# Attention loop of a gated block: TensorE's side work split into halves over two steps, with a new step table

## The chip, the cores and the metric

The kernel runs on one core of a Trainium2 chip. The metric is the device time of one execution in microseconds (us). All times below are in us unless marked ns. The engines are TensorE (PE; its weight loads are PEld), VectorE (DVE), ScalarE (ACT), GpSimd (POOL) and SyncE (SP, which issues most of the DMAs).

## What is computed

```python
x = x + tanh(g_xattn) * attention(layernorm(x), ctx, ctx, Wq, Wk, Wv, Wo)   # 16 heads, 512 queries, 1601 keys
x = x + tanh(g_ffn) * moe(layernorm(x), router_w, w1, w2)                    # top 2 of 8 experts

# attention: the softmax runs over the queries (axis=2), then each row is divided by its sum over the keys
attn = einsum("bhnc,bhlc->bhnl", qh * scale, kh)
attn = softmax(attn, axis=2)
attn = attn / sum(attn, axis=-1, keepdims=True)
out = einsum("bhnl,bhlc->bhnc", attn, vh)
```

x is 8 x 512 x 256, ctx is 8 x 1601 x 256, everything in float32.

## The kernel before

It has two phases. The first, `attention_and_routing`, takes the 8 batches one after the other; the second, `experts`, runs 71 blocks of 128 routed rows through their expert. The change touches the first alone.

**Steps.** A batch has 52 steps (`STEPS` = 4 groups of 4 heads x 13 tiles of 128 keys). A step has two units, one for each pair of heads. For a unit TensorE computes two scores tiles of 128x512 (L549) into one of three slots of PSUM; VectorE takes their negated maximum over the queries (L810); ScalarE computes the two exponentials with their sums (L659). Once a step VectorE takes the reciprocals of the four sums (L796), GpSimd scales the values with them (L934), and TensorE adds the weighted values into `acc` (L562), two steps behind the scores. The scores of a unit wait for the exponentials of the unit three before it.

**Side work.** TensorE also has 31 "fills" per batch, each into the one PSUM bank `spare`, and each in the step that the table `FILL_AT` gives it, between the scores of the step's first and second unit. "next" fills prepare the following batch: `k` 0 to 7 and `q` 0 and 1 are projections of two fp32 matmuls (L493, L483), `v` 0 to 6 projections of four (L499; the last has two), `x_turn` are transposes of x (L478). "tail" fills finish the batch before: `o_turn` 3, `attn_turn` 1, `out_proj` 0 and 1 (eight PE instructions each at L512), `row_turn`, `logits`, `prefix`. "cur" fills belong to the batch itself. In the loop over batches the first has no tail and the last has no next; b is 0 to 7.

**Who empties the bank.** A fill waits until the fill before it has been taken (`fill_taken`). `k` and `q` are taken by ScalarE at the start of their step, before the step's first exponential (L606, high part as bf16), then by VectorE after the maximum of the step's second unit (L711, remainder), and by GpSimd (two more parts, the last one a step later). `v` and `x_turn` are taken by ScalarE at the start of the step (L615, L619). `o_turn`, `attn_turn`, `out_proj` (L726), `row_turn`, `logits` and `prefix` are taken by VectorE between the maxima of the step's first and second unit.

**Queues.** The parts of k and q go to DRAM through two buffers in turn: SyncE stores them (L359, L354), and ScalarE's high part of a chunk waits until the store of the chunk two before has landed. SyncE's queue is in order: at the start of a batch it issues 16 loads of the fourth group's operands (L366, L368), then the stores of k 0 to 3, the store of x2, the stores of k 4 to 7, loads of x, the store of q 0, the loads for group 1 of the next batch, the store of q 1, the loads for groups 2 and 3, and last the load of the context of the batch after the next (L379), which waits until `v` 6 has been taken. `k` 0 waits for that load. For the first batch the loads of groups 2, 3 and 4 stand together ahead of the store of its k 0.

Of the kernel before, what the change touches and what calls it, by code (L numbers as in the profile page):

```python
# [40 lines left out]
KC = D // P  # L41
NT = N // P
LT = (L + P - 1) // P
# [23 lines left out]


FILL_AT = {
    2: ("next", "k", 0), 3: ("tail", "o_turn", 3), 4: ("next", "k", 1), 5: ("tail", "attn_turn", 1),  # L70
    6: ("tail", "out_proj", 0), 7: ("next", "k", 2), 8: ("tail", "out_proj", 1), 9: ("next", "k", 3),
    11: ("next", "k", 4), 13: ("next", "k", 5), 15: ("next", "k", 6), 16: ("cur", "o_turn", 0),
    17: ("tail", "row_turn", 0), 18: ("tail", "row_turn", 1), 20: ("tail", "logits", 0), 21: ("next", "k", 7),
    22: ("next", "x_turn", 0), 23: ("next", "x_turn", 1), 24: ("next", "q", 0), 26: ("next", "q", 1),
    28: ("next", "v", 0), 29: ("next", "v", 1), 30: ("cur", "o_turn", 1), 31: ("next", "v", 2),
    33: ("next", "v", 3), 35: ("next", "v", 4), 36: ("tail", "prefix", 0), 37: ("next", "v", 5),
    39: ("next", "v", 6), 42: ("cur", "o_turn", 2), 43: ("cur", "attn_turn", 0),
}


FIRST_FILL_AT = {s + 21: ("next", name, i) for s, (name, i) in enumerate(
# [2 lines left out]
ORDER = [KC + i for i in range(KC * KCHUNK)] + list(range(KC))  # L84
FIRST_ORDER = [KC + i for i in range(KCHUNK)] + [0] + [KC + i for i in range(KCHUNK, 2 * KCHUNK)] + [1]
EARLY = KCHUNK + 1
LOGITS = 20
ROUTE = 23
PLACE = 37
OUT = 8  # L90
STATS_X = (7, 11, 12, 13)
CENTRE_X = 16


class Iteration:
# [22 lines left out]
    def fill(self, s):  # L118

        if s not in self.table:  # L120
            return None
        kind, name, i = self.table[s]
        return (name, i) if {"tail": self.tail, "cur": self.cur, "next": self.next}[kind] else None

    def two_banks(self, name, i):

# [61 lines left out]
def attention_and_routing(nc, keep, x, ctx_t, g_xattn, g_ffn, wq_t, wk_t, wv_t, wo_t, router_t,  # L188
# [7 lines left out]
    with ExitStack() as ctx:  # L196
# [265 lines left out]
        def _(pe):  # L462
            pe.wait_ge(constants, 1)

            def fill(it, name, i):
                b = it.b
                spare = bank(it, name, i)
                if it.two_banks(name, i):

                    wait(pe, fill_taken, it.made(name, i) - 2)  # L470
                elif name != "logits":

                    wait(pe, fill_taken, it.made(name, i) - 1)
                if name == "x_turn":

                    pe.wait_ge(xn_ready, 2 * (b + 2))
                    for t in range(NT):
                        mm = pe.transpose(spare[:, t * P:(t + 1) * P], x_in[:, t, i * P:(i + 1) * P], ident[:, :])  # L478
                elif name == "q":
                    if it.first and i == 0:  # L480
                        pe.wait_ge(weights_in, N_WEIGHTS * 16)
                    for k in range(KC):
                        mm = pe.matmul(spare[:, :], wq_sb[:, k, i * P:(i + 1) * P], x_t[:, k, :],  # L483
                                       start=(k == 0), stop=(k == KC - 1))
                elif name == "k":
                    m, c = i // KCHUNK, i % KCHUNK
                    if it.first and i == 0:

                        pe.wait_ge(wk_in, 16)
                    if i == 0:  # L490
                        pe.wait_ge(ctx_loaded, (b + 2) * 16)
                    for k in range(KC):
                        mm = pe.matmul(spare[:, 0:KCOLS[c + 1] - KCOLS[c]], wk_sb[:, k, m * P:(m + 1) * P],  # L493
                                       ctx_sb[:, k, KCOLS[c]:KCOLS[c + 1]], start=(k == 0), stop=(k == KC - 1))
                elif name == "v":
                    for lt in range(2 * i, min(2 * i + 2, LT)):
                        r = rows_of(lt)
                        for k in range(KC):
                            mm = pe.matmul(spare[0:r, (lt % 2) * D:(lt % 2 + 1) * D], ctx_sb[:, k, lt * P:lt * P + r],  # L499
                                           wv_sb[:, k, :], start=(k == 0), stop=(k == KC - 1))  # L500
                elif name == "o_turn":

                    pe.wait_ge(acc_taken, b * G + i + 1 if i < G - 1 else b * G)
                    for t in range(NT):
                        mm = pe.transpose(spare[:, t * P:(t + 1) * P], o_acc[:, t * P:(t + 1) * P], ident[:, :])
                elif name == "attn_turn":
                    for t in range(NT):
                        mm = pe.transpose(spare[:, t * P:(t + 1) * P], attn[:, t, i * P:(i + 1) * P], ident[:, :])
                elif name == "out_proj":
                    for t in (2 * i, 2 * i + 1):  # L510
                        for k in range(KC):
                            mm = pe.matmul(spare[:, (t % 2) * D:(t % 2 + 1) * D], attn_t[:, k, t * P:(t + 1) * P],  # L512
                                           wo_sb[:, k, :], start=(k == 0), stop=(k == KC - 1))
                elif name == "row_turn":

                    pe.wait_ge(rows_ready, 2 * b)
                    for t in range(NT):
                        mm = pe.transpose(spare[:, t * P:(t + 1) * P], routed_rows[:, 0, t, i * P:(i + 1) * P], ident[:, :])
                elif name == "logits":
                    for t in range(NT // 2, NT):  # L520
                        for k in range(KC):
                            mm = pe.matmul(spare[:, t * E:(t + 1) * E], row_t[:, k, t * P:(t + 1) * P],
                                           router_sb[:, k, :], start=(k == 0), stop=(k == KC - 1))
                else:

                    pe.wait_ge(route_step, b * ROUTE_STEPS)
                    pe.matmul(spare[:, 0:NT * E], tri[:, :], chosen[:, :, :], start=True, stop=False)
                    mm = pe.matmul(spare[:, 0:NT * E], ones[:, :], seen_at[:, :, :], start=False, stop=True)
                mm.then_inc(fill_ready, 1)

            def first_logits(it):

# [33 lines left out]
            def run(it):  # L566
                for s in range(STEPS):
                    if s == SLOTS // 2 and it.cur and isinstance(it.b, int) and it.b == 0:

                        pe.wait_ge(fill_taken, it.base)  # L570
                    if it.cur:
                        unit_scores(it.b, s, 0)
                    if it.fill(s):
                        fill(it, *it.fill(s))
                    if it.tail and s == LOGITS - 1:
                        first_logits(it)
                    if it.cur:
                        unit_scores(it.b, s, 1)
                    if s >= 2 and it.cur:
                        weigh(it.b, s - 2)  # L580
                    if s < 2 and it.tail:
                        weigh(it.b - 1, STEPS + s - 2)
# [678 lines left out]
```

## Time and profile before

| what | value |
|---|---|
| median of 3 runs | 1903.37 us (1903.24 to 1906.2) |
| profiled execution | 1903.8 us, its span 1902.0 us |
| PE busy | 1672.8 us, 88% of the span |
| DVE busy | 1407.2 us, 74% |
| ACT busy | 1289.1 us, 68% |
| POOL busy | 557.8 us, 29% |
| batch loop | from 56 us to 1311 us |
| expert phase | to the end of the span |

The shares are means over two phases with different limits: in the second half of the span PE alone is busy nearly all the time, in the batch loop three engines are. A stretch of the loop is read from a table of windows, which has the busy time of each engine in it.

### The profile page before, as it was taken

The numbers are of one execution on the slowest core, as the hardware profiler recorded it, in microseconds if no ns is written. First come the engines' busy times: TensorE is split into PE (matmuls) and PEld (weight loads), VectorE is DVE, ScalarE is ACT, GpSimd is POOL, SyncE is SP. The second block draws the span as 40 slices with busy tenths as digits, with TensorE's granted clock in tenths as the row PEclk, the third lists the DMA queues.
The fourth block names the chain that finished last, engine by engine and source line by source line (L and its number), as shares of the span: only waits on it lengthen the run. The fifth ranks groups of instructions, "written<-read, shape, count | busy, mean of one in ns | idle before, by whom it ended". The sixth has DMA issues, their size and how long they took to land. (4 is left out here: it accounts for less than half of the span.)

```text
span 1902.0 us, 31292 instructions
## 1 busy us (share of the span) xinstructions
PE 1672.8 (88%) x9774; PEld 889.5 (47%) x9888; DVE 1407.2 (74%) x2269; ACT 1289.1 (68%) x3634; POOL 557.8 (29%) x837
## 2 busy tenths in 40 slices
PE   5589899889988989989988898886299999999997
PEld 3223233233323323323322332212299999999997
DVE  1488999999989999899998999996344444444443
ACT  2499989989999998999999999995011111111111
POOL 5141152235135135223413512213212222222222
PEclk9799999999999999999999999998599999999999
DMA  5915414432522441532343152114512222222221
GB/s 152 228 35 142 120 56 117 119 89 85 155 80 71 136 130 51 133 121 77 97 143 80 56 150 73 45 67 157 198 31 36 36 36 36 38 34 38 36 36 28
DMA packets 124933, 168.64 MB, mean 89 GB/s; under 512 B 14320, under 2 KB 102256, under 8 KB 124816
## 3 DMA queue, kind: packets, MB, share of 16 engines
q1 hardware_dynamic: 102064, 136.77, 26.1%
q0 software_dynamic: 13344, 17.90, 5.5%
q10 hardware_dynamic: 9408, 12.58, 1.8%
q8 instruction: 53, 0.87, 0.2%
q14 instruction: 64, 0.52, 0.1%
HBM read 117.96 MB, written 49.24 MB: 88 GB/s over the span
## 5 line engine op out<-in xcount | busy, mean ns | idle before, releaser
L659 ACT ACTIVATE w_all<-scores,negmax 128x512 f32<-128x512 f32 (+1 forms) x1664 | 1120.3, 717 | 48.6 <-DVE negmax L810 42.4
L810 DVE TENSOR_REDUCE negmax<-scores 128x2 f32<-128x1024 f32 (+1 forms) x832 | 1000.6, 1215 | 105.0 <-PE scores L549 100.4
L549 PE MATMUL scores<-q_stack,w_all 128*128 128x512 bf16 (+1 forms) x1550 | 477.8, 385 | 131.6 <-ACT w_all L659 114.2
L562 PE MATMUL acc<-w_all,vz 128*32 128x512 f32 (+1 forms) x3328 | 445.0, 607 | 8.8 <-POOL vz L934 7.7
L549 PEld LDWEIGHTS scores<-q_stack,w_all 128*128 128x128 bf16 (+1 forms) x1664 | 112.8, 100 | 605.4 <-ACT w_all L659 460.1
L659 ACT ACTIVATION_READ_ACCUMULATOR w_all<-scores,negmax 128x1 f32 (+1 forms) x1664 | 393.0, 236 | 0.0
L1128 ACT ACTIVATE hidden<-ps_hidden 128x512 f32<-128x512 f32 x142 | 84.8, 597 | 430.0 <-PE ps_hidden L1091 430.0
L934 POOL TENSOR_TENSOR vz<-w_all,rz 128x68 f32<-128x68 f32 (+1 forms) x416 | 124.6, 299 | 835.3 <-DVE rz L796 816.6
L1091 PEld LDWEIGHTS ps_hidden<-rows_t,w_sb 128*128 128x128 f32 x2272 | 267.4, 194 | 5.7 <-DVE rows_t L1155 1.7
L1091 PE MATMUL ps_hidden<-rows_t,w_sb 128*128 128x128 f32 x2272 | 268.2, 277 | 1.1 <-DVE rows_t L1155 1.0
L1104 PE MATMUL ps_y<-w_sb,hidden 128*128 128x256 f32 x1136 | 256.8, 379 | 0.0
L1206 POOL DMA_INDIRECT out<-result,gate_token x71 | 119.5, 1683 | 415.5 <-DVE result L1168 406.2
L1104 PEld LDWEIGHTS ps_y<-w_sb,hidden 128*128 128x128 f32 x1136 | 210.4, 190 | 25.7
L562 PEld LDWEIGHTS acc<-w_all,vz 128*32 128x32 f32 (+1 forms) x3328 | 65.5, 108 | 188.2 <-issue 117.0
L1161 DVE COPY gate_token<-rows 128x2 f32<-128x2 f32 x71 | 12.0, 170 | 181.2 <-DMA out<-result,gate_token 181.2
L493 PE MATMUL spare<-w_all,wk_sb 128*128 128x400 f32 (+1 forms) x240 | 94.0, 515 | 16.7 <-DMA w_all<-in_ctx_t 15.2
L1168 DVE TENSOR_SCALAR result<-ps_y,gate_token 128x256 f32<-128x256 f32 x71 | 34.4, 484 | 96.3 <-PE ps_y L1104 96.3
L1145 DVE COPY w_sb<-w_all 128x2048 f32 x71 | 86.9, 1224 | 14.5 <-POOLq L1199 14.2
L499 PE MATMUL spare<-wv_sb,w_all 128*128 128x256 f32 (+1 forms) x392 | 93.5, 380 | 2.1 <-DVE resid L711 1.5
L1150 DVE COPY w_sb<-w_all 128x2048 f32 x71 | 86.5, 1218 | 0.0
L499 PEld LDWEIGHTS spare<-wv_sb,w_all 128*128 128x128 f32 (+1 forms) x392 | 72.6, 186 | 19.1 <-DVE resid L711 2.3
L992 POOL DMA_INDIRECT routed<-routed_rows,place x64 | 65.0, 1015 | 28.8 <-DVE token L789 15.3
(134 smaller groups left out, 1008.2 us busy)
## 6 DMA issues: line engine op xcount, KB each, us to landing
w_all<-k_parts SPq DMA_DIRECT2D x256, 200.1 KB, 3.5
q_stack<-q_parts SPq DMA_DIRECT2D x256, 64.0 KB, 3.3
w_all<-in_ctx_t SPq DMA_DIRECT2D x8, 1601.0 KB, 7.9
k_parts<-parts SPq DMA_DIRECT2D x42, 300.0 KB, 2.8
w_all<-in_w ACTq DMA_DIRECT2D x12, 1024.0 KB, 12.0
rows<-routed SPq DMA_DIRECT2D x71, 129.0 KB, 2.0
q_parts<-parts SPq DMA_DIRECT2D x14, 384.0 KB, 3.1
k_parts<-parts SPq DMA_DIRECT2D x14, 300.8 KB, 3.0
```

Of the source, the lines that this page charges most:

```text
L493: mm = pe.matmul(spare[:, 0:KCOLS[c + 1] - KCOLS[c]], wk_sb[:, k, m * P:(m + 1) * P], ctx_sb[:, k, KCOLS[c]:KCOLS[c + 1]], start=(k == 0), ...
L499: mm = pe.matmul(spare[0:r, (lt % 2) * D:(lt % 2 + 1) * D], ctx_sb[:, k, lt * P:lt * P + r], wv_sb[:, k, :], start=(k == 0), stop=(k == KC ...
L549: mm = pe.matmul(scores[0:r, 2 * (u % SLOTS) + j % 2, :], k_stack[:, g, j, lt * P:lt * P + r], q_stack[:, g, j, :], start=True, stop=True)
L562: mm = pe.matmul(acc[32 * j:32 * j + 32, :], vz[0:r, s % RING, j, :], probs[0:r, s % RING, j, :], start=(lt == 0), stop=(lt == LT - 1))
L659: e = act.activation(probs[0:r, s % RING, j, :], scores[0:r, 2 * (u % SLOTS) + j % 2, :], ACT.Exp, bias=negmax[0:r, u % 4, j % 2:j % 2 + 1 ...
L810: dve.tensor_reduce(negmax[0:r, u % 4, :], scores[0:r, 2 * (u % SLOTS):2 * (u % SLOTS) + 2, :], AX.X, ALU.max, negate=True).then_inc(negma ...
L934: pool.tensor_tensor(vz[0:r, s % RING, :, 0:DH + 1], v_ones[0:r, b % 2, lt, g * GH:(g + 1) * GH, :], rz[0:r, s % RING, :].unsqueeze(2).to_ ...
L1091: mm = pe.matmul(ps_hidden[:, slot * BANKS + h // HB, (h % HB) * BLK:(h % HB + 1) * BLK], w1_sb[:, slot, k * HID + h * P:k * HID + (h + 1) ...
L1104: mm = pe.matmul(ps_y[:, slot, 0:D], hidden[:, slot, h * BLK:(h + 1) * BLK], w2_sb[:, slot, h * D:(h + 1) * D], start=(h == 0), stop=(h == ...
L1145: dve.tensor_copy(w1_sb[:, slot, :], w1_all[:, bass.ds(e * (KC * HID), KC * HID)]).then_inc(w1_ready, 1)
L1150: dve.tensor_copy(w2_sb[:, slot, :], w2_all[:, bass.ds(e * (HC * D), HC * D)]).then_inc(w2_ready, 1)
L1206: pool.indirect_dma_start(out=out, out_offset=bass.IndirectOffsetOnAxis(gate_token[:, slot, 1:2].bitcast(U32), 0), in_=result[:, slot, :], ...
```

## The change

The fills `k`, `q`, `v` (all but the last) and `out_proj` are issued in two halves: the first in the step before the one of the table, the second in the step of the table, each between the two units' scores. The wait for the bank stands before the first half. The first pass (b = -1, which has no attention beside it) keeps whole fills. The table is new: `k` 0 and 1 move from steps 2 and 4 to 1 and 3, `out_proj` from 6 and 8 to 7 and 9, `k` 2 to 5 from 7, 9, 11 and 13 to 11, 13, 15 and 18, `k` 6 and 7 from 15 and 21 to 24 and 26, `q` from 24 and 26 to 31 and 33, `v` 0 to 6 from 28..39 to 35..47. The steps of routing and of the statistics move one or two steps back with it.

```diff
 FILL_AT = {
-    2: ("next", "k", 0), 3: ("tail", "o_turn", 3), 4: ("next", "k", 1), 5: ("tail", "attn_turn", 1),
-    6: ("tail", "out_proj", 0), 7: ("next", "k", 2), 8: ("tail", "out_proj", 1), 9: ("next", "k", 3),
-    11: ("next", "k", 4), 13: ("next", "k", 5), 15: ("next", "k", 6), 16: ("cur", "o_turn", 0),
-    17: ("tail", "row_turn", 0), 18: ("tail", "row_turn", 1), 20: ("tail", "logits", 0), 21: ("next", "k", 7),
-    22: ("next", "x_turn", 0), 23: ("next", "x_turn", 1), 24: ("next", "q", 0), 26: ("next", "q", 1),
-    28: ("next", "v", 0), 29: ("next", "v", 1), 30: ("cur", "o_turn", 1), 31: ("next", "v", 2),
-    33: ("next", "v", 3), 35: ("next", "v", 4), 36: ("tail", "prefix", 0), 37: ("next", "v", 5),
-    39: ("next", "v", 6), 42: ("cur", "o_turn", 2), 43: ("cur", "attn_turn", 0),
+    1: ("next", "k", 0), 3: ("next", "k", 1), 4: ("tail", "o_turn", 3), 5: ("tail", "attn_turn", 1),
+    7: ("tail", "out_proj", 0), 9: ("tail", "out_proj", 1), 11: ("next", "k", 2), 13: ("next", "k", 3),
+    15: ("next", "k", 4), 16: ("cur", "o_turn", 0), 18: ("next", "k", 5), 19: ("tail", "row_turn", 0),
+    20: ("tail", "row_turn", 1), 22: ("tail", "logits", 0), 24: ("next", "k", 6), 26: ("next", "k", 7),
+    27: ("next", "x_turn", 0), 28: ("next", "x_turn", 1), 29: ("cur", "o_turn", 1), 31: ("next", "q", 0),
+    33: ("next", "q", 1), 35: ("next", "v", 0), 37: ("next", "v", 1), 38: ("tail", "prefix", 0),
+    40: ("next", "v", 2), 42: ("next", "v", 3), 44: ("next", "v", 4), 46: ("next", "v", 5),
+    47: ("next", "v", 6), 48: ("cur", "attn_turn", 0), 49: ("cur", "o_turn", 2),
 }
+HALVED = ("k", "q", "v", "out_proj")
...
-LOGITS = 20
-ROUTE = 23
-PLACE = 37
-OUT = 8
+LOGITS = 22
+ROUTE = 25
+PLACE = 39
+OUT = 9
 STATS_X = (7, 11, 12, 13)
-CENTRE_X = 16
+CENTRE_X = 17
...
+    def halves(self, s):
+
+        now, after = self.fill(s), self.fill(s + 1)
+        if self.first:
+            return [(now, (0, 1))] if now else []
+        begun = after and after[0] in HALVED and after != ("v", VF - 1)
+        assert not (begun and now) or now[0] in HALVED
+        if now:
+            split = now[0] in HALVED and now != ("v", VF - 1)
+            return [(now, (1,) if split else (0, 1))]
+        return [(after, (0,))] if begun else []
...
-            def fill(it, name, i):
+            def fill(it, name, i, halves):
...
-                if it.two_banks(name, i):
+                if 0 not in halves:
+                    pass
+                elif it.two_banks(name, i):
...
-                    for k in range(KC):
+                    for k in halves:
...
-                    for lt in range(2 * i, min(2 * i + 2, LT)):
+                    for lt in (2 * i + h for h in halves if 2 * i + h < LT):
...
-                    for t in (2 * i, 2 * i + 1):
+                    for t in (2 * i + h for h in halves):
...
-                mm.then_inc(fill_ready, 1)
+                if 1 in halves:
+                    mm.then_inc(fill_ready, 1)
...
-                    if it.fill(s):
-                        fill(it, *it.fill(s))
+                    for f, halves in it.halves(s):
+                        fill(it, *f, halves)
```

## Rows read from the trace of the kernel before

**Rows 1.** The page: the span, and busy time of each engine.
```profile
span 1902.0 us, 31292 instructions
PE 1672.8 (88%) x9774; PEld 889.5 (47%) x9888; DVE 1407.2 (74%) x2269; ACT 1289.1 (68%) x3634; POOL 557.8 (29%) x837
```

**Rows 2.** Windows: batch 3; its steps 1 to 20; 21 to 51; steps 45 to 49; batches 7, 0.
```profile
core 0: us, PE busy (x) PEld busy (x) DVE busy (x) ACT busy (x) POOL busy (x), PEclk, DMA share, GB/s
540.67:697.69 157.02, 141.46 (x781) 49.43 (x798) 144.74 (x235) 150.23 (x437) 54.42 (x94) 1.00 0.37 104
543.46:606.66 63.20, 57.83 (x314) 21.76 (x316) 59.82 (x96) 58.02 (x168) 30.65 (x48) 1.00 0.22 62
606.66:697.69 91.03, 80.85 (x453) 27.24 (x464) 82.36 (x136) 89.42 (x262) 23.48 (x45) 1.00 0.46 128
678.20:691.46 13.26, 10.41 (x67) 1.94 (x60) 12.13 (x16) 13.26 (x43) 6.86 (x11) 1.00 0.15 52
1168.76:1310.79 142.03, 117.37 (x683) 30.18 (x695) 136.36 (x215) 140.16 (x417) 30.98 (x68) 1.00 0.18 58
56.23:226.64 170.41, 137.47 (x713) 42.74 (x730) 135.18 (x182) 149.23 (x435) 38.83 (x77) 0.93 0.48 122
```

**Rows 3.** Timeline of batch 3, step 8 (out_proj 1); in brackets idle time and its releaser.
```profile
564.15 1.21 DVE L810 TENSOR_REDUCE negmax<-scores 128x2 f32<-128x1024 f32 x1
564.29 1.99 PE L512 MATMUL spare<-wo_sb,attn_t 128*128 128x256 f32 x8 [0.33 <-DVE resid L711]
566.32 0.75 DVE L726 SCALAR_TENSOR_TENSOR x<-spare,tgx,x 128x512 f32<-128x512 f32 x1 [0.96 <-PE spare L512]
566.99 1.21 DVE L810 TENSOR_REDUCE negmax<-scores 128x2 f32<-128x1024 f32 x1
568.24 0.69 ACT L659 ACTIVATE w_all<-scores,negmax 128x512 f32<-128x512 f32 x1 [1.39 <-DVE negmax L810]
```

**Rows 4.** Timeline of batch 3, steps 21 and 22: k 7, then x_turn 0.
```profile
604.54 0.60 PE L549 MATMUL scores<-q_stack,w_all 128*128 128x512 bf16 x2
...
604.98 1.51 PE L493 MATMUL spare<-w_all,wk_sb 128*128 128x401 f32 x4
...
606.33 0.59 PE L549 MATMUL scores<-q_stack,w_all 128*128 128x512 bf16 x2
...
607.85 0.60 PE L549 MATMUL scores<-q_stack,w_all 128*128 128x512 bf16 x2
608.10 0.17 DVE L796 RECIPROCAL rz<-z 128x4 f32<-128x4 f32 x1
608.19 0.55 DVE L711 SCALAR_TENSOR_TENSOR resid<-spare,parts 128x401 f32<-128x401 f32 x1
...
608.65 1.21 DVE L810 TENSOR_REDUCE negmax<-scores 128x2 f32<-128x1024 f32 x1
...
608.79 0.66 PE L478 MATMUL spare<-ident,x_in 128*128 128x128 f32 x4 [0.33 <-DVE resid L711]
```

**Rows 5.** Timeline of ACT in batch 3, about the high part of k 0.
```profile
546.13 0.51 ACT L606 ACTIVATE parts<-spare 128x400 bf16<-128x400 f32 x1
546.51 0.71 ACT L659 ACTIVATE w_all<-scores,negmax 128x512 f32<-128x512 f32 x1
```

**Rows 6.** Timeline of batch 0: context, k 0, step 3 on ACT, the store of k 0, k 2.
```profile
53.54 0.37 SPq L379 DMA_DIRECT2D w_all<-in_ctx_t  x1
...
62.89 3.01 PE L493 MATMUL spare<-w_all,wk_sb 128*128 128x400 f32 x4 [2.79 <-DMA w_all<-in_ctx_t]
...
70.66 0.69 ACT L659 ACTIVATE w_all<-scores,negmax 128x512 f32<-128x512 f32 x1 [1.16 <-DVE negmax L810]
...
87.25 19.88 SPq L359 DMA_DIRECT2D k_parts<-parts  x4
93.43 0.51 ACT L606 ACTIVATE parts<-spare 128x400 bf16<-128x400 f32 x1 [11.55 <-DMA k_parts<-parts]
```

**Rows 7.** SP's queue at the end of batch 3, and landing times of the context loads.
```profile
668.56 0.58 SPq L379 DMA_DIRECT2D w_all<-in_ctx_t  x1
693.77 0.53 SPq L366 DMA_DIRECT2D q_stack<-q_parts  x1
DMA to landing us min/median/max: 6.8/7.9/9.6
```

**Rows 8.** Waits of ACT in steps 1 to 20 of batch 3, then in batch 7.
```profile
ACT w_all L659 <- DVE negmax L810: 4.9, 9, 1.4
ACT w_all L659 <- DVE negmax L810: 1.9, 5, 0.7
```

More of the change, by code:

```diff
@@ L491, in fill @@
                         pe.wait_ge(ctx_loaded, (b + 2) * 16)
-                    for k in range(KC):
+                    for k in halves:
                         mm = pe.matmul(spare[:, 0:KCOLS[c + 1] - KCOLS[c]], wk_sb[:, k, m * P:(m + 1) * P],
```

## Prediction

> **What bounds the kernel now.** The page first [rows 1]: PE is busy 88% of the span, but that is a mean over two phases, and the change reaches only the batch loop. So I read windows of one batch. Batch 3 lasts 157.02 us; ACT is busy 150.23 of them, DVE 144.74, PE 141.46 [rows 2]. Three engines near full: none has much to give, and the time is set by which is late where. Five steps without side work take 13.26 us, 2.65 each, with ACT busy throughout and DVE idle 0.23 a step [rows 2]: that is ACT's floor, 52 x 2.65 = 137.8. What ACT takes from fills comes on top (a high part of k costs it 0.38, from 546.13 to 546.51 [rows 5]).
>
> Cut the batch in two. In steps 21 to 51 ACT is busy 89.42 of 91.03: ACT-bound, little to win. In steps 1 to 20 ACT is busy 58.02 of 63.20 and DVE 59.82 [rows 2]. Here most of the tail's work sits on DVE, and ACT waits 4.9 us for maxima [rows 8]. The floor of this stretch is DVE's work, and the loss over it is 63.20 - 59.82 = 3.4 us.
>
> Where that comes from is seen in step 8 [rows 3]. DVE must take out_proj before the second maximum. PE begins the whole fill at 564.29 and DVE sits idle 0.96 until it is done; take and maximum follow, and ACT stands 1.39.
>
> **The change, part by part.** The fills' instructions are the same in number and kind; the sum of work stays. Only places change.
>
> *Shorter fills.* A whole k fill holds PE from 604.98 to the scores at 606.33, 1.35 us, before the second unit's scores [rows 4]. A half holds it for 0.68. For out_proj and v half of 1.99 is left out of a step, about 0.9 net. So the second unit's maximum can start 0.7 to 0.9 earlier, and out_proj is ready for DVE about 0.9 earlier: its waits of 0.96 in step 8, and what the same pattern costs in step 6, go. They are covered then by DVE's own first maximum, 1.21 long [rows 3].
>
> *The new wait.* The bank must be free a step earlier. k's taker is DVE's L711, which comes behind the second maximum. In steps 21 and 22 the fill after k already stands in the next step, and PE waits 0.33 there [rows 4], with the scores before it delayed by the whole fill. In the new table this holds for k 0, 2, 3 and 6, whose following half stands in the very next step, and for k 1, 4, 5 and 7 ahead of a transpose. Behind the waiting half, on PE, are the scores of the second unit and the weighted sum; for those scores wait DVE, then ACT.
>
> I followed steps 0 to 20 with pitches from start to start: maximum 1.15, reciprocal 0.09 (608.10 to 608.19), L711 0.46 (to 608.65) [rows 4], other takes of DVE 0.60 to 0.67 (566.32 to 566.99 [rows 3]), a unit on ACT 1.325 (2.65 / 2), k on ACT 0.38. PE: 0.44 from scores to a fill, half fill 0.68, 0.5 scores to weighted sum, 1.0 for that. An example, step 12: DVE, which in step 11 has two statistics of x2, one of x and k 2, ends the remainder of k 2 about 2.0 after PE could begin the half of k 3; the next maximum is late too, and ACT stands about 1.2. The longest waits of PE come out as 1.1 (k 1), 2.0 (k 3), 1.8 (k 4), 0.5 to 0.9 before the transposes, some 7 us per batch; most lie beside DVE's own work, which is the bound here anyway. In the middle of the stretch DVE never runs dry. The result is 61.1 us for steps 1 to 20 against 63.20, a gain of 2.1. That is DVE's work there less k 6 and the logits, which leave the stretch (59.82 - 0.46 - 0.35 = 59.0), and 2.1 of gaps where 3.4 were.
>
> *Steps 21 to 51.* k 6 comes in: +0.38 on ACT. ACT's waits here, 91.03 - 89.42 = 1.6, of which about 0.7 stand at the batch boundary (104 units do not divide by three slots, unchanged), shrink with the half fills of q and v by about 0.4. v is taken by ACT at the start of its step, so its half in the next step finds the bank free. Net 0. Per batch: -2.1, for six batches (1 to 6) -12.6. Bounds: no gain at all where the new waits eat it (0), and all of DVE's idle time gone (3.4 a batch, 20).
>
> *Batch 7* has the tail but no k: of its 1.9 us of ACT waits [rows 8] those behind out_proj go, -0.7 (bounds 0 and 1.9).
>
> *Batch 0* is a case of its own: 170.41 us although it has no tail [rows 2]. Two stalls. First, k 0 waits for the context, issued at 53.54 and usable at 62.89 [rows 6]. Before, k 0 stood behind the scores of five units (step 2); now its first half stands behind the first (step 0). PE is released at the same 62.89, but with four units fewer done. It restarts at the slow clock as it did before (the fill took 3.01 against 1.51 [rows 4, 6]; the window's granted clock is 0.93 [rows 2]). By the pitches, at the slow clock, ACT comes to step 3 some 11.6 us after the release, at 74.5 instead of 70.66 [rows 6]: +4; at most four units, 5.3. Second, k 2's high part waits 11.55 us for a buffer, because the store of k 0 stands behind SyncE's 48 loads and issues only at 87.25, free at 93.43 [rows 6]. k 2 moves from step 7 to step 11. From 74.5, with eight steps at 2.65 and the high part of k 1, ACT comes to k 2 at about 96, after 93.43: the 11.55 go entirely. PE's idle time there also cost a slow restart, about 2 us. Sum: +4 - 11.6 - 2.4 = -10. Bounds: -6 (the dear end of the first, no restart gained) and -12.
>
> *The context of later batches.* v 6 is taken in step 47 instead of 39, k 0 wanted in step 0 instead of 2. Taking v 6 ends about 13.6 us before the batch's end (5 steps, the boundary's 0.9, less the copy), PE wants k 0 about 1.4 before it: 12.2 us of room. Landing took 6.8 to 9.6 [rows 7]. SyncE must be free: it issues store q 0, group 1, store q 1, groups 2 and 3, about 38 us from q 0's store on; with q 0 in step 31 that ends some 18 us before the end. Next in its queue are the 16 loads of group 4, at 693.77 before [rows 7], unmoved. Cost nothing, 2.6 us to spare in the worst landing seen; the 8 row scatters beside it are new company.
>
> The store of x2 now issues after k 3's, some four steps later; its reload is wanted a batch later: nothing waits. GpSimd is busy 30.65 of 63.20 [rows 2], its row work moves one step with the tail, the values it scales are wanted a step later: nothing.
>
> **Sum.** 1903.8 - 12.6 - 0.7 - 10 = 1880.5 for an execution like the profiled one; the median of the runs is 0.4 below it. Forecast 1880.
>
> **Rivals.**
> A. *The waits eat the gain* in batches 1 to 6. For it: one bank, eight fills right behind a k where the old table has five, waits up to 2 us long by my count. Against: the count has DVE busy meanwhile. Left are batch 0 and 7: 1903.4 - 10.7 = 1893. The Trainium skill, Perfetto Trace Analysis, section Matmuls, says that independent groups should rotate through different PSUM banks so that taking one overlaps the next; opening the next group earlier in the same bank gains nothing by it, which is this rival. The trace agrees as far as a wait of 0.33 behind L711 stands there [rows 4]; it is short.
> B. *Slower: the waits fall on the chain.* Place: the half fill after L711, then scores, maximum, exponential. Price: 7 us per batch if PE's waits pass to ACT whole, less 2.1 of gain already counted: 1903.4 + 4.9 x 6 - 10.7 = 1922. It decides from about 4.5 of the 7 us reaching ACT. Against it: DVE has 2 to 3 us of work in hand then, and ACT has up to 0.7 us of finished maxima.
> C. *Batch 0's stall stays*, if the store of k 0 frees its buffer later: -12.6 - 0.7 + 4 gives 1894. Against: its issue hangs on SyncE's queue alone.
> D. *The context comes late*: from a landing over 12.2 us on, each us costs 6 in all; slower than before only from 17 us on, against 9.6 as the longest.
>
> **Chances.** Forecast 0.57, A 0.22, B 0.1, C 0.08, D 0.03. The predicted time is the forecast's. 1866 (3.4 per batch, 12, 1.9: 1903.4 - 34.3 = 1869, and 3 for pitches taken long) to 1896 (A with -6 in batch 0 gives 1896.7) leaves out B, D and the rims. A measurement of this kernel tells apart some 0.2%, 3.8 us. Faster 0.84 (forecast, A, C less their rims), same 0.06, slower 0.1.
>
> **What would show it.** After the change: DVE's wait for L512 before L726 is gone; batch 0 has no wait of L606 for a store and lasts about 160; the wait for the context stands in step 0, 9 us long; PE's waits for L711 grow to some 5 us a batch; batch 3 lasts about 155. The forecast is wrong if ACT's waits for maxima do not fall below 4.9 in steps 1 to 20, or if a PE wait for the context appears in later batches.

## The result, and the profile after

| | before | after |
|---|---|---|
| median | 1903.66 (1903.24 to 1906.2) | 1862.33 (1860.44 to 1863.45) |
| profiled execution, span | 1903.8, 1902.0 | 1863.19, 1861.3 |
| batch 0 | 170.41 | 158.14 |
| batches 1 to 6, each | 157.02 | 152.56 |
| batch 7 | 142.03 | 141.18 |
| the rest, from the loop's end | 591.2 | 590.3 |

The ratio is 0.9779, with a 95% interval of 0.9762 to 0.9796: 2.2% faster. Forecast were 1880, and 1866 to 1896 as the range: the sign was right, and the gain was larger than the range allowed. Batch lengths are read from the first exponential's start of one batch to that of the next; batch 7 ends 0.68 after the start of its last exponential. The gain of 40.7 in the span is 12.3 in batch 0, six times 4.46 (26.8), 0.85 in batch 7 and 0.9 behind the loop. The forecast had 10, six times 2.1 (12.6), 0.7 and nothing. So most of what is missing, 14 of 17.5, is missing in batches 1 to 6, which are alike.

The page after, to be read against [rows 1]: the work is the same, and only the span is shorter.

```profile
span 1861.3 us, 31293 instructions
PE 1665.0 (89%) x9775; PEld 892.7 (48%) x9888; DVE 1408.8 (76%) x2269; ACT 1281.1 (69%) x3634; POOL 557.7 (30%) x837
```

Windows after, the same stretches as in [rows 2]: batch 3, its steps 1 to 20, its steps 21 to 51, batch 7, batch 0.

```profile
core 0: us, PE busy (x) PEld busy (x) DVE busy (x) ACT busy (x) POOL busy (x), PEclk, DMA share, GB/s
519.55:672.10 152.55, 140.42 (x781) 49.94 (x799) 144.92 (x234) 149.09 (x436) 54.38 (x94) 1.00 0.40 107
522.60:582.06 59.46, 53.77 (x306) 18.62 (x304) 58.31 (x94) 57.02 (x166) 28.75 (x46) 1.00 0.22 60
582.06:672.10 90.04, 83.60 (x465) 30.42 (x474) 83.79 (x138) 89.02 (x264) 25.34 (x48) 1.00 0.51 134
1129.80:1270.99 141.19, 117.54 (x684) 30.16 (x696) 135.88 (x215) 140.01 (x417) 31.04 (x68) 1.00 0.18 58
56.30:214.43 158.13, 136.03 (x719) 43.34 (x736) 137.70 (x183) 148.18 (x435) 38.84 (x77) 0.97 0.52 134
```

Steps 1 to 20 went from 63.20 to 59.46, where 61.1 was forecast. Steps 21 to 51 went from 91.03 to 90.04, where 91.0 was forecast; and k 6 did come in, with its 0.38. Step 0 grew from 2.79 to 3.05: k 0 now stands in steps 0 and 1, and its high part (0.38 on ACT) comes just ahead of step 1's first exponential. The first stretch before ends 0.39 ahead of the first exponential of step 21 (607.05), so that k 7's high part is in the second stretch there, as it is after. DVE is now busy 58.31 of 59.46 in the first stretch and ACT 89.02 of 90.04 in the second: by the busy shares each stretch has an engine that hardly stands.

The line numbers shift by 15 or 16: L711 is now L727, L726 is L742, L606 is L622, L659 is L675, L810 is L826. Waits of batch 3 after, in the form: engine, line, releaser, us in total, times, longest.

```profile
PE spare L508 <- DVE resid L727: 3.6, 4, 1.2
ACT w_all L675 <- DVE negmax L826: 2.7, 7, 0.7
PE spare L520 <- DVE resid L727: 1.0, 2, 0.6
PE spare L493 <- DVE resid L727: 0.5, 1, 0.5
PE spare L498 <- DVE resid L727: 0.4, 1, 0.4
PE spare L514 <- DVE resid L727: 0.4, 1, 0.4
PE spare L533 <- DVE resid L727: 0.4, 1, 0.4
```

Six groups of PE stand behind the remainder of k or q, together 6.3 where before they were 1.7. The 4.6 between them is the new wait. ACT waits 2.7 in the whole batch, and of that 1.8 in steps 1 to 20, where 4.9 stood [rows 8].

The pattern of [rows 3] after, out_proj 1, now step 9:

```profile
543.97 1.03 PE L527 MATMUL spare<-wo_sb,attn_t 128*128 128x256 f32 x4
544.25 1.20 DVE L826 TENSOR_REDUCE negmax<-scores 128x2 f32<-128x1024 f32 x1
545.36 0.74 DVE L742 SCALAR_TENSOR_TENSOR x<-spare,tgx,x 128x512 f32<-128x512 f32 x1
546.01 1.22 DVE L826 TENSOR_REDUCE negmax<-scores 128x2 f32<-128x1024 f32 x1
```

The second half takes PE 1.03 instead of 1.99 and is done at 545.00, while DVE still takes the first maximum. L742 follows it without the 0.96 of idle time, and the second maximum follows that.

### The profile page after: what moved, and what is told of

Same layout as the page of the kernel before. It is cut to its first block and busy times, and to the rows that moved or that the text cites. A ratio compares the mean times of both kernels' runs of the same rounds, so it can differ in the third digit from the quotient of the medians.

```text
span 1861.3 us, 31293 instructions
## 1 busy us (share of the span) xinstructions
PE 1665.0 (89%) x9775; PEld 892.7 (48%) x9888; DVE 1408.8 (76%) x2269; ACT 1281.1 (69%) x3634; POOL 557.7 (30%) x837
## 3 DMA queue, kind: packets, MB, share of 16 engines
q1 hardware_dynamic: 102064, 136.77, 26.8%
## 5 line engine op out<-in xcount | busy, mean ns | idle before, releaser
L675 ACT ACTIVATE w_all<-scores,negmax 128x512 f32<-128x512 f32 (+1 forms) x1664 | 1126.8, 753 | 33.3 <-DVE negmax L826 27.5
L826 DVE TENSOR_REDUCE negmax<-scores 128x2 f32<-128x1024 f32 (+1 forms) x832 | 1001.6, 1215 | 81.5 <-PE scores L565 74.3
L675 ACT ACTIVATION_READ_ACCUMULATOR w_all<-scores,negmax 128x1 f32 (+1 forms) x1664 | 453.6, 273 | 0.0
L508 PE MATMUL spare<-w_all,wk_sb 128*128 128x400 f32 (+1 forms) x240 | 107.1, 532 | 45.4 <-DVE resid L727 25.9
L514 PE MATMUL spare<-wv_sb,w_all 128*128 128x256 f32 (+1 forms) x392 | 101.1, 382 | 5.2 <-DVE resid L727 4.6
L508 PEld LDWEIGHTS spare<-w_all,wk_sb 128*128 128x128 f32 x240 | 44.6, 196 | 75.7 <-DVE resid L727 41.2
```

The costliest lines, as they stand in the source:

```text
L675: e = act.activation(probs[0:r, s % RING, j, :], scores[0:r, 2 * (u % SLOTS) + j % 2, :], ACT.Exp, bias=negmax[0:r, u % 4, j % 2:j % 2 + 1 ...
L826: dve.tensor_reduce(negmax[0:r, u % 4, :], scores[0:r, 2 * (u % SLOTS):2 * (u % SLOTS) + 2, :], AX.X, ALU.max, negate=True).then_inc(negma ...
```

## Experiments

Each row is one kernel; "batch" is the length of those of batches 1 to 6 that are free of the clock event told last (the 142.57 of batch 7 in e10 has it). Batch lengths are of the profiled execution. Ratios are to the kernel before, measured beside it.

| kernel | median | ratio (95%) | batch 0 | batch | batch 7 |
|---|---|---|---|---|---|
| before | 1903.66 | 1 | 170.41 | 157.02 | 142.03 |
| e1 new table, no halves | 1886.19 | 0.9902 (0.9885 to 0.9918) | 160.72 | 155.60 | 142.11 |
| e2 old table, halves | 1910.62 | 1.0034 (1.0022 to 1.0047) | 172.70 | 157.45 | 141.91 |
| e3 halves of out_proj only | 1877.66 | 0.9862 (0.9845 to 0.9878) | 158.62 | 154.44 | 141.19 |
| e10 halves of v and out_proj | 1870.03 | 0.9822 (0.9807 to 0.9837) | 160.33 | 153.27 | 142.57 |
| e4 first half after unit 2's scores | 1878.53 | 0.9866 (0.9849 to 0.9882) | 157.76 | 155.00 | 142.16 |
| e5 k 0 whole | 1869.37 | 0.9818 (0.9801 to 0.9834) | 157.25 | 153.29 | 141.29 |
| e6 before, stores of k first in batch 0 | 1896.89 | 0.9961 (0.9947 to 0.9975) | 165.41 | 156.97 | 141.92 |
| after | 1862.33 | 0.9779 (0.9762 to 0.9796) | 158.14 | 152.56 | 141.18 |
| e7 after, other steps for the statistics | 1859.62 | 0.9764 (0.9748 to 0.9780) | 157.14 | 152.31 | 141.29 |
| e8 after, six more fills whole | 1856.92 | 0.9754 (0.9738 to 0.9771) | 157.40 | 151.68 | 141.28 |
| e9 e8 with e7 | 1855.34 | 0.9748 (0.9735 to 0.9762) | 156.52 | 151.40 | 141.18 |

### The table alone, the halves alone

e1, against the kernel after:

```diff
-HALVED = ("k", "q", "v", "out_proj")
+HALVED = ()
```

> The new table with whole fills (nothing halved). Theory 1, the shorter fills earn most in batches 1 to 6: DVE's waits for out_proj come back (about 0.3 and 0.3 to 1.0 us) and so do the small late takes of v; a batch of 155 to 156 us where the changed kernel has 152.6 and the old one 157.0; in all about 1880. Theory 2, the new places earn it and the halves add nothing: a batch within 0.5 of 152.6, in all 1862 to 1866. Both expect batch 0 without the wait for k 0's store, 155 to 159 us, since k 2 stands in step 11 either way; with k 0 whole in step 1 its wait for the context comes behind three units instead of one, so 1 to 2 us less than the changed kernel's 158.1.

e2, against the kernel before: `FILL_AT` stays, and fills are halved only where the old table has the step before free. These are k 0, 4, 5, 6, q 1, v 3, v 4 and v 0, which the expectation overlooked.

```diff
+HALVED = ("k", "q", "v", "out_proj")
...
+        def split(f, at):
+            return f and f[0] in HALVED and f != ("v", VF - 1) and (at - 1) not in self.table
+        if now:
+            return [(now, (1,) if split(now, s) else (0, 1))]
+        return [(after, (0,))] if split(after, s + 1) else []
```

> The old table, with halves only for the fills whose step before is free: k 0, 4, 5 and 6, q 1, v 3 and v 4. out_proj stays whole. Theory 1: a pair of steps with v falls from 5.9 to 5.77 us (twice), the ACT waits at k 4, k 6 and q 1 (0.49, 0.45, 0.31) fall: 1 to 1.5 us less per batch, about 155.7, in all 1894 to 1897. Theory 2: halves earn nothing without the table, 157.0 a batch and 1903. Batch 0 keeps its wait of about 11.5 us for the store of k 0 by both.

The table alone gives 1.42 a batch, as Theory 1 of e1 had it (its total came out 6 above the 1880). The halves that the old table has room for cost 0.43, where e2's expectation had a gain of 1 to 1.5, and together the table and all halves give 4.46. The parts don't add, but it is no clean sum either: e2 halves only 8 of the 18 pieces, and not out_proj. The new table is what makes free steps for the others. But a free step isn't enough, the bank must be empty too. The halves of k 0 leave steps 0 to 2 at 8.52, as before. Steps 13 to 15, where k 6's first half comes right behind k 5, are 0.24 longer, and steps 27 and 28, where v 0's comes right behind q 1, are 0.47 longer. Timeline of e2, batch 3, step 27:

```profile
628.86 1.13 PE L514 MATMUL spare<-wv_sb,w_all 128*128 128x256 f32 x4 [0.44 <-DVE resid L727]
...
631.72 0.69 ACT L675 ACTIVATE w_all<-scores,negmax 128x512 f32<-128x512 f32 x1 [0.20 <-DVE negmax L826]
```

PE waits 0.44 for the remainder of q 1, and ACT then stands 0.20 for a maximum; step 27 takes 3.54 instead of 3.13. With the halves of v 3 and v 4, which wait for nothing, steps 32 to 35 are 0.41 shorter, of which step 36 gives 0.16 back.

### Which halves pay

e3 has `HALVED = ("out_proj",)`:

> The new table, with out_proj alone in halves. Theory 1a, what the halves earn is DVE's idle time ahead of out_proj: a batch within 0.5 of 152.6. Theory 1b, it is spread over all fills (v alone seven times 0.14 us by the steps): a batch of 154 to 155, in all 1870 to 1877. The difference to the run with nothing halved is out_proj's part.

e10 has `HALVED = ("v", "out_proj")`:

> The new table with v and out_proj in halves, k and q whole. Against the run with out_proj alone (154.4 a batch) it gives v's part. Theory (v's hidden waits, seven takes of v of 0.14 us and the step of o_turn 2): steps 39 to 50 fall from 35.5 to 34.3, a batch of 153.0 to 153.4, in all 1866 to 1872, some batches again 1.6 longer by the clock at the batch boundary since k 0 is whole. Rival (k and q earn it): 154.4 within 0.3, in all 1877.

With e1 and the kernel after they make a ladder for a batch: 155.60 with none, 154.44 with out_proj (-1.16), 153.27 with v (-1.17), 152.56 with k and q as well (-0.71). Out_proj gives most of its part in steps 6 to 10: 15.12 against 14.15. v gives its part in steps 39 to 50, which hold v 2 to 6. Windows over these steps, of e3 and then of e10:

```profile
640.43:675.91 35.48, 33.49 (x194) 12.78 (x188) 31.40 (x46) 34.76 (x104) 10.72 (x19) 1.00 0.75 191
```

```profile
639.03:673.29 34.26, 32.74 (x192) 11.95 (x184) 31.93 (x46) 34.26 (x104) 10.75 (x19) 1.00 0.73 198
```

In e3 ACT is busy 34.76 of 35.48, which looks full. In e10 it is busy all of 34.26. So 1.22 of a stretch in which ACT was 98% busy could be had. The trace of e3 marks 0.72 as idle, in three waits for maxima. How much of the 1.22 that is shows only when ACT's exponentials are laid beside each other in the two runs, from start to start. The three pairs with the marked waits are 0.83 longer in e3 (0.42, 0.39 and 0.03). The five intervals with a copy in them are 0.22 longer; there the copies come 3.49 after their exponentials instead of 3.31. The other pairs are 0.16 longer in all, 0.08 of it in one of step 44 (0.75 instead of 0.66). So 0.4 stands in no wait and counts as busy. The third pair, in step 49, tells why. From start to start it takes 0.95 in e3 with 0.17 marked idle, and 0.92 in e10 with none marked. e10 at that pair:

```profile
668.38 0.92 ACT L675 ACTIVATE w_all<-scores,negmax 128x512 f32<-128x512 f32 x1
668.95 0.44 ACT L675 ACTIVATION_READ_ACCUMULATOR w_all<-scores,negmax 128x1 f32 x1
669.30 0.69 ACT L675 ACTIVATE w_all<-scores,negmax 128x512 f32<-128x512 f32 x1
```

The second exponential is 0.26 late against the pitch of 0.66, and the booked 0.44 of the accumulator read (0.21 in e3) covers the gap. The kernel before shows the same in batch 3, v 1:

```profile
629.61 1.89 PE L499 MATMUL spare<-wv_sb,w_all 128*128 128x256 f32 x8
630.66 0.73 ACT L659 ACTIVATE w_all<-scores,negmax 128x512 f32<-128x512 f32 x1
631.23 0.25 ACT L659 ACTIVATION_READ_ACCUMULATOR w_all<-scores,negmax 128x1 f32 x1
631.53 0.59 ACT L615 COPY w_all<-spare 128x512 f32<-128x512 f32 x1
632.01 0.69 ACT L659 ACTIVATE w_all<-scores,negmax 128x512 f32<-128x512 f32 x1
```

The fill ends at 631.50 and the copy starts at 631.53: ACT's copy waited for PE, and no idle time is marked on it. From the exponential to the copy it is 0.87, where 0.66 is the pitch without a wait. The same pair and the next exponential in the kernel after:

```profile
627.95 0.74 ACT L675 ACTIVATE w_all<-scores,negmax 128x512 f32<-128x512 f32 x1
628.61 0.65 ACT L631 COPY w_all<-spare 128x512 f32<-128x512 f32 x1
629.08 0.77 ACT L675 ACTIVATE w_all<-scores,negmax 128x512 f32<-128x512 f32 x1
```

0.66 to the copy, 0.47 from it. Over the batch, what each v fill adds to ACT's start-to-start times is 0.47, 0.69, 0.47, 0.59, 0.49, 0.55, 0.26 before (v 0 to 6) and six times 0.47 and 0.25 after.

### Where the first half stands

e4 puts the first halves behind the scores of the step's second unit; the second halves stay.

```diff
                     for f, halves in it.halves(s):
-                        fill(it, *f, halves)
+                        if 1 in halves:
+                            fill(it, *f, halves)
...
                     if it.cur:
                         unit_scores(it.b, s, 1)
+                    for f, halves in it.halves(s):
+                        if 1 not in halves:
+                            fill(it, *f, halves)
```

> The changed kernel with the first half of a fill issued behind the scores of the second unit instead of ahead of them. PE's waits for the remainder of k (6.3 us per batch in the trace after) then no longer hold back those scores. Theory: the waits lie beside DVE's own work and cost nothing: a batch within 0.3 of 152.6; batch 0 about 1.5 us shorter, since one more unit stands ahead of the wait for the context; in all about 1860. Rival, the waits fall on the chain in part: a batch 1 us or more shorter, in all 1855 or less.

It loses 2.4 a batch, which neither side of the expectation had, although asking for the bank later does shorten PE's waits for the remainder, from 6.3 to 2.0 in batch 3. The likely reason is the place: both halves then stand between the scores of the step's second unit and those of the next step's second unit, with one unit's scores between them, so for that second unit nearly the whole fill is back in one piece. The step lengths bear it out for v: steps 39 to 50 take 35.49, as with whole fills (35.48 in e1), where the kernel after takes 34.25. For out_proj, steps 6 to 10 take 14.85, near e1's 15.12 and not the 13.98 of after. Of the 3.04 a batch that the halves give over e1, 0.60 are left. PE's waits at the bank are cheaper here than a fill that stands together.

### What the new waits cost

e8 leaves whole those fills of the kernel after whose first half stands right behind a k or q that DVE has still to take:

```diff
+WHOLE = (("v", VF - 1), ("k", 1), ("k", 3), ("k", 4), ("k", 7), ("q", 1), ("v", 0))
...
-        begun = after and after[0] in HALVED and after != ("v", VF - 1)
+        begun = after and after[0] in HALVED and after not in WHOLE
...
-            split = now[0] in HALVED and now != ("v", VF - 1)
+            split = now[0] in HALVED and now not in WHOLE
```

> The changed kernel with those fills whole whose first half would stand right behind a k or q that VectorE has still to take: k 1, 3, 4 and 7, q 1, v 0. Theory 1, those waits cost (steps 2, 14, 32 and 34 are 0.2 to 0.3 us longer than with whole fills): about 1 us per batch less, 151.6, in all 1857. Theory 2, the waits lie beside VectorE's own work, and what the halves earn elsewhere is lost with them: 152.4 to 153, in all 1862 to 1865.

A batch is 0.88 shorter. The largest parts: step 2 goes from 3.28 to 3.05, step 4 from 3.06 to 2.66, step 14 from 3.35 to 3.05, steps 32 to 34 from 9.80 to 9.53. PE's waits for the remainder fall from 6.3 to 1.6. So 4.7 of waits are gone, and what that gained, less what the six halves had earned, is 0.9. The two parts can't be told apart here.

e5 leaves only k 0 whole, in step 1:

```diff
-        begun = after and after[0] in HALVED and after != ("v", VF - 1)
+        begun = after and after[0] in HALVED and after not in (("v", VF - 1), ("k", 0))
...
-            split = now[0] in HALVED and now != ("v", VF - 1)
+            split = now[0] in HALVED and now not in (("v", VF - 1), ("k", 0))
```

> The changed kernel with k 0 whole in step 1, all else in halves. Theory 1 (the first half of k 0 keeps TensorE at work at the batch boundary): some batches lose 1.6 us in step 0 to a granted clock of 0.5, as in the run with nothing halved; the others are about 0.4 longer than 152.6 or equal. In all 1863 to 1870. Rival (the boundary has nothing to do with it, the slow batches came from elsewhere): all six batches alike. Batch 0: k 0's wait for the context stands behind three units instead of one: steps 0 to 2 about 2.7 us shorter by that (8.3 + 3.4 + 3.1 in the run with nothing halved, 11.2 + 3.0 + 3.3 here), but k 2 is then reached earlier than 93.4 us and its wait for the store comes back in part, 1 to 3 us: batch 0 about as long as now.

A batch is 0.73 longer, steps 0 to 5 taking 18.76 instead of 18.11, and one of its six batches (154.93) has the clock event, as Theory 1 had it. So the half of k 0 in step 0 pays in each later batch, although it costs in batch 0, where steps 0 to 5 take 25.38 with it and 23.42 without.

e7 moves statistics of x out of the steps in which DVE has k's remainder as well:

```diff
-STATS_X = (7, 11, 12, 13)
+STATS_X = (2, 6, 8, 12)
```

> The changed kernel with the four statistics of x in steps 2, 6, 8 and 12 instead of 7, 11, 12 and 13, where VectorE has the statistics of x2 and two k as well. Theory: in steps 1 to 20 VectorE's work in its order is the bound, so taking it out of the crowded steps 11 and 13 earns up to 0.7 us per batch (the wait of ACT in step 11 is 0.73): a batch of 151.9 to 152.3, in all 1858 to 1861. Rival: the stretch is bound by the sum of VectorE's work, not by its order; 152.6 within 0.1.

It gives 0.25 a batch of the up to 0.7 expected: step 11 goes from 3.58 to 3.25 (step 9 grows by 0.32, steps 13 and 14 shrink). So the order of DVE's work counts there, and not its sum alone. This was the stall that the forecast put at 1.2, in step 12; ACT's wait measured 0.73, in step 11. e9 has the edits of e7 and e8:

> The changed kernel with k 1, 3, 4 and 7, q 1 and v 0 whole, and the four statistics of x in steps 2, 6, 8 and 12: the two edits that earned, together. If they do not touch each other, a batch is 151.67 - 0.25 = 151.4 and the whole 1854 to 1856. If both took the same idle time of VectorE's order in steps 11 to 15, a batch stays at 151.7 and the whole at 1857.

The two gains add (0.88 and 0.25; 1.16 measured), and e9 beats both kernels: 1855.34 against 1862.33 and 1903.66. Windows of batch 3 in e9:

```profile
515.34:666.73 151.39, 142.01 (x796) 49.98 (x799) 144.44 (x234) 148.58 (x436) 54.34 (x94) 1.00 0.40 108
```

### Batch 0 and SyncE's queue

e6 changes only the kernel before, and only in batch 0: the loads of group 4 go behind the stores of k 0 to 3 instead of ahead of them.

```diff
-                    load_stacks(b, 3)
+                    if not (isinstance(b, int) and b == 0):
+                        load_stacks(b, 3)
...
                         store_parts(it, c)
+                    if isinstance(b, int) and b == 0:
+                        load_stacks(b, 3)
```

> The kernel before, with the 16 loads of group 4 of batch 0 issued behind the stores of its k 0 to 3 instead of ahead of them; nothing else. Theory: the 11.55 us wait of batch 0 is SyncE's queue alone. k 0's store issues some 10 us earlier, so 10 of the 11.55 go, and the slow restart in step 8 (4.83 us) goes with it: batch 0 at 158 to 160 instead of 170.4, in all 1891 to 1894. Rival: the store's landing is what is late (the DMA engines are full of loads), and the time stays within 3 us of 1903.

It gained less than expected, 5.0 in batch 0 where 10 to 12 stood. Timeline of e6, batch 0, k 2 and then k 6:

```profile
75.89 22.36 SPq L359 DMA_DIRECT2D k_parts<-parts  x4
84.11 0.50 ACT L609 ACTIVATE parts<-spare 128x400 bf16<-128x400 f32 x1 [3.55 <-DMA k_parts<-parts]
...
113.18 0.50 ACT L609 ACTIVATE parts<-spare 128x400 bf16<-128x400 f32 x1 [3.53 <-DMA k_parts<-parts]
```

The store issues 11.4 earlier (75.89 against 87.25 [rows 6]), and the wait at k 2 falls from 11.55 to 3.55. But the 16 moved loads now stand ahead of k 4's store, and the buffer that k 6 needs comes 3.53 late. Nor does the slow restart go: step 8 takes 5.28 (4.83 before) at a mean granted clock of 0.61, after the shorter wait too. The cause of the stall is shown, the queue's order; the size of the gain was a miss, since 16 loads moved in an ordered queue delay whoever is behind them.

## Why the forecast was wrong, step by step

Two terms of the sum failed, and both lie in batches 1 to 6. In steps 0 to 20 the forecast had a gain of 2.1 and 3.5 was measured; in steps 21 to 51 it had none and 1.0 was measured. The first was too small, the second wrong in its premise.

**Steps 21 to 51: the premise that failed.** The forecast read "ACT is busy 89.42 of 91.03: ACT-bound, little to win", and net 0, from 0.38 for k 6 and 0.4 less of waits. The stretch gained 0.99, which is 1.37 without k 6. ACT's idle time fell from 1.61 to 1.02, by 0.6 where 0.4 was forecast. The rest, 0.8, came out of its busy time: 89.42 with k 6 would be 89.80, and 89.02 was measured. That is the part that the busy share hid, short delays that carry no idle time. e3 against e10 shows this for v; for the rest of the stretch it was not taken apart. e1 tells what the forecast had too small: the stretch takes 91.58 with the table alone, so the halves are worth 1.5 in it, where they were counted at 0.4, and the table costs 0.5, of which k 6 is 0.38. The Trainium skill, Perfetto Trace Analysis, section Identifying the Most-Contended Engine, holds busy time to be a fair measure for ScalarE of how near it is to its limit. It names the right engine here, and yet a stretch of 35.5 at 98% had 1.2 to give, of which the share shows 0.7.

**Steps 1 to 20: right in kind, mis-sized.** The stretch gained 3.7 instead of 2.1; less the 0.26 that step 0 grew, for which the sum has no term, it is 3.5. The wait ahead of L726 is gone, and ACT's waits for maxima fell from 4.9 to 1.8. The forecast was 61.1, as 59.0 of DVE's work and 2.1 of gaps; 59.46 came, as 58.31 busy and 1.15 of gaps. So both parts were too large, the gaps by 0.95 and the work by 0.7. 0.5 of it is the stand of ACT beside k 2 and its statistics (1.2 forecast, 0.73 measured). The 0.7 of work was not taken apart. It may be booked time again: DVE's instructions too are booked longer than their pitch, so that a sum of busy time over a stretch with many short gaps overstates the work. Timeline of batch 3 after:

```profile
549.55 0.72 DVE L845 BATCH_NORM_STATS2 stats<-x 128x6 f32<-128x256 f32 x2
550.19 1.21 DVE L826 TENSOR_REDUCE negmax<-scores 128x2 f32<-128x1024 f32 x1
```

The two statistics are booked to 550.27 and the maximum begins at 550.19. The prediction had allowed 3 for "pitches taken long", over the whole kernel; that was too little. Of the 3.7, e1 has 2.5 with the table alone (60.74 for the stretch), so the halves gave the smaller part here. Together the two stretches, less step 0's 0.26, make 4.46 where 2.1 stood.

**The new waits: right.** 6.3 a batch (some 5 forecast as seen in a profile, 7). Rival B, that they pass to ACT whole, is refuted, since ACT waits less than before. Rival A, that they eat the gain, is refuted as a forecast, but e8 shows that it isn't empty: with six fills whole a batch is 0.9 shorter. Two of the waits, of 0.4 each, stand behind the remainder of q, which the forecast's count of eight leaves out. The Trainium skill, Perfetto Trace Analysis, section Matmuls, says that independent groups should rotate through different PSUM banks, so that taking one overlaps the matmuls of the next. The 6.3 that PE waits here at one bank agree with it. What a rotation would gain no run shows: a second bank wasn't tried, and e8's 0.9 is net of what its six halves had earned, so it is no bound.

**Batch 0: right in both terms, and 0.3 past the bound of -12.** Forecast -10, measured -12.3. Timeline of batch 0 after, k 0's first half, the exponential behind it, and k 2's high part:

```profile
61.92 1.67 PE L508 MATMUL spare<-w_all,wk_sb 128*128 128x400 f32 x2 [7.00 <-DMA w_all<-in_ctx_t]
...
65.75 0.69 ACT L675 ACTIVATE w_all<-scores,negmax 128x512 f32<-128x512 f32 x1 [8.00 <-DVE negmax L826]
...
94.92 0.73 ACT L622 ACTIVATE parts<-spare 128x400 bf16<-128x400 f32 x1
```

The wait for the context stands in step 0 (7.0, forecast 9), step 3 begins at 73.74 (74.5 forecast, 70.66 before): a loss of 3.1, where 4 was forecast. The stall of 11.55 at k 2 is gone, against rival C. It is gone by little: k 2 comes at 94.9, and in the kernels with k 0 or all of k whole a rest of it stands. The waits for the store at k 2 are 2.78 in e1, 1.04 in e3, 3.34 in e10 and 1.26 in e5:

```profile
95.47 0.50 ACT L622 ACTIVATE parts<-spare 128x400 bf16<-128x400 f32 x1 [2.78 <-DMA k_parts<-parts]
```

Batch 0 is 160.72 in e1 and 158.62 in e3, which issue the same in it, so its length is known to some 2 only. The 2.3 beyond the forecast are 1.0 of smaller loss in steps 0 to 2, 0.8 in steps 3 to 20 (14.8 gained, 14.0 forecast) and 0.5 in steps 21 to 51 (90.48 to 89.99), where the forecast had nothing, as in the later batches.

**The rest.** Rival D didn't come: batches 1 to 6 have no wait of PE for the context. SyncE's queue at the end of batch 3 after, against [rows 7]:

```profile
658.08 0.38 SPq L392 DMA_DIRECT2D w_all<-in_ctx_t  x1
668.13 0.53 SPq L379 DMA_DIRECT2D q_stack<-q_parts  x1
```

The context issues 14.0 ahead of the batch's end, as was reckoned (v 6 taken 13.6 ahead of it), and SyncE is back at the next loads 4.0 ahead of it. Batch 7 gained 0.85 (0.7 forecast); it is 142.11 in e1 and 141.19 in e3, so it is the halves of out_proj, as forecast. The 0.9 behind the loop is no effect of the change that could be told from scatter: that phase is the same in all twelve kernels, and it lasted between 588.2 and 591.2 in their profiled executions.

**Left open.** Whether a second bank would turn the waits into gain; which fills other than v hid waits in steps 21 to 51; why batch 0 scatters by 2.

## What to carry to other kernels

An engine that is busy 98% of a stretch can still be waiting, in pieces that its booked durations cover; lay the start-to-start times of one kind of instruction beside the shortest of them, and what is over it is where to look. Splitting a piece of side work over two steps pays where the step before is free and the buffer already empty, and costs where its first half must wait for the taker of the piece before: split by piece, not by kind, and try the table and the split both alone and together. In a queue that issues in order, moving the work that waits to a later point took away a stall that moving the transfers only took away in part, and in part passed on to a later store.

## What the runs showed that was not expected

Some batches ran part of their first steps at the lower TensorE clock (a granted clock of 0.50 from 218 to 220 in e1, so 1.2 GHz and not 2.4). e1, the start of batch 1 and then that of batch 3, the same stretch of work:

```profile
217.12:222.00 4.88, 4.88 (x20) 1.61 (x21) 2.53 (x3) 3.15 (x9) 0.30 (x1) 0.65 0.84 206
```

```profile
531.61:534.90 3.29, 3.29 (x20) 1.21 (x22) 2.52 (x3) 3.20 (x10) 0.29 (x1) 1.00 0.87 249
```

The stretches differ by the mean granted clock, 0.65 against 1.00, and 20 instructions of PE take 4.88 instead of 3.29. Such a batch is 1.65 longer (157.25 against 155.60). PE stands twice ahead of it, at the batch boundary:

```profile
215.23 0.59 PE L565 MATMUL scores<-q_stack,w_all 128*128 128x512 bf16 x2 [1.13 <-ACT w_all L675]
216.47 0.61 PE L565 MATMUL scores<-q_stack,w_all 128*128 128x512 bf16 x2 [0.65 <-ACT w_all L675]
```

Among batches 1 to 6 it came in 5 of the 24 of e1, e3, e5 and e10, in which k 0 is whole in step 1, in 2 of 6 in e2, where k 0's halves stand in steps 1 and 2, and in none of the 30 of the kernel after, e4, e7, e8 and e9, where half of k 0 stands in step 0. It also came in batch 7 of e10, which has no k 0 at all. In the kernel after the second of the two waits is then not there; PE, the start of its batch 3:

```profile
517.66 0.59 PE L565 MATMUL scores<-q_stack,w_all 128*128 128x512 bf16 x2 [1.13 <-ACT w_all L675]
518.09 0.83 PE L508 MATMUL spare<-w_all,wk_sb 128*128 128x400 f32 x2
518.91 0.61 PE L565 MATMUL scores<-q_stack,w_all 128*128 128x512 bf16 x2
```

So it seems that part of what the halves of k give in a whole execution is this, and it isn't in the 0.71 of the ladder: two such batches are 3.3 of e1's profiled execution. But the kernel before and e6, with k 0 whole in step 2, had none in 12, so a half in step 0 isn't needed to be free of it. The same two waits stand ahead of e1's batch 3, which ran at the full clock; why one batch falls and another doesn't stays open.

The booked duration of ACT's instructions is no constant, and tells more than their cost. In e10 it rises through steps 39 to 49, here from v 2's copy to v 5's, while the times from start to start stay at 0.57, 0.09 and 0.47:

```profile
641.02 0.75 ACT L675 ACTIVATE w_all<-scores,negmax 128x512 f32<-128x512 f32 x1
641.59 0.27 ACT L675 ACTIVATION_READ_ACCUMULATOR w_all<-scores,negmax 128x1 f32 x1
641.68 0.65 ACT L631 COPY w_all<-spare 128x512 f32<-128x512 f32 x1
...
658.36 0.86 ACT L675 ACTIVATE w_all<-scores,negmax 128x512 f32<-128x512 f32 x1
658.93 0.38 ACT L675 ACTIVATION_READ_ACCUMULATOR w_all<-scores,negmax 128x1 f32 x1
659.02 0.76 ACT L631 COPY w_all<-spare 128x512 f32<-128x512 f32 x1
```

In e3 the exponentials of these steps stand at 0.68 to 0.73, and its waits come in between (0.29, 0.26, 0.17). In e10 itself they rise to 0.92 and fall to 0.69 right behind the late exponential at 669.30. The longer booking goes with an engine that has not waited for long, the shortest with one that just did. That is a reading of these kernels and wasn't tested by itself, but it says why a sum of booked durations can't be laid against a span.
